# Second message-passing layer, sorted edges: node sums stored plainly by SyncE, the border node carried by a one-row matmul

## The reference

```python
hid = silu(edge_scalars @ fc_w1 * _inv(R))              # R = 64
w = hid @ fc_w2 * _inv(FC_HID)                          # 224 weights per edge
w1, w2, w3, w4, w5 = split(w, [64, 128, 160, 192], axis=-1)
es, ev = h_s[edge_src], h_v[edge_src]                   # rows gathered by source node
e0, e1 = edge_attr[:, :1], edge_attr[:, 1:4]
m_s1 = w1 * es * e0
m_s2 = w4 * einsum('eci,ei->ec', ev, e1) * _inv(3)
m_v1 = (w2 * es)[:, :, None] * e1[:, None, :]
m_v2 = w3[:, :, None] * ev * e0[:, :, None]
m_v3 = w5[:, :, None] * cross(ev, e1[:, None, :]) * _inv(2)
agg_s = segment_sum(concatenate([m_s1, m_s2], -1), edge_dst, n)     # 96 numbers per node
agg_v = segment_sum(concatenate([m_v1, m_v2, m_v3], 1), edge_dst, n)  # 128 x 3 per node
```

## Time and profile before

| | |
|---|---|
| runs, median (lowest, highest) | 3804.27 us (3803.56, 3806.49) |
| the profiled execution | 3801.2 us |
| its span, first to last instruction | 3799.6 us |
| TensorE busy | 3507.5 us (92%) |
| VectorE busy | 3493.0 us (92%) |
| ScalarE busy | 3048.0 us (80%) |
| GpSimd busy | 2571.1 us (68%) |
| mean granted TensorE clock | 0.978 |

### The profile page before, as it was taken

How to read it: one execution, slowest core, us unless ns; L and a number is a source line. 1 busy time by engine, 2 the same in 40 slices (tenths; PEclk the granted TensorE clock), 3 DMA queues, 4 the chain that set the end, 5 groups by cost and what they waited for, 6 DMA issues and landing times. The chain is left out here.

```text
span 3799.6 us, 96198 instructions
## 1 busy us (share of the span) xinstructions
PE 3507.5 (92%) x21340; PEld 2637.2 (69%) x21340; DVE 3493.0 (92%) x11954; ACT 3048.0 (80%) x11217; POOL 2571.1 (68%) x2474
## 2 busy tenths in 40 slices
PE   4999999999999999999999957977999999999997
PEld 3888888888888888888888847875333333333335
DVE  5999999999999999999999987876999999999995
ACT  4888888888888888888888856765878777878774
POOL 1777777777777777777777721112777777777772
PEclk8999999999999999999999978997999999999999
DMA  4333333333333333333333359982333433343434
GB/s 111 90 97 96 93 98 94 94 97 94 95 96 94 96 94 94 97 95 94 96 96 93 97 159 264 274 239 69 94 95 95 96 94 95 96 94 94 96 94 116
DMA packets 311032, 414.62 MB, mean 109 GB/s; under 512 B 112692, under 2 KB 245684, under 8 KB 310708
## 3 DMA queue, kind: packets, MB, share of 16 engines
q0 software_dynamic: 127568, 211.04, 24.8%
q1 hardware_dynamic: 183396, 202.83, 17.0%
HBM read 312.70 MB, written 100.94 MB: 109 GB/s over the span
## 5 line engine op out<-in xcount | busy, mean ns | idle before, releaser
L669 POOL DMA_INDIRECT ACC<-src_tab,idx x784 | 832.9, 1062 | 312.2 <-issue 238.6
L669 POOL DMA_INDIRECT TAB<-dst_tab,idx x784 | 829.2, 1058 | 238.9 <-issue 238.9
L736 POOL DMA_INDIRECT ACC<-hid_tab,idx x784 | 808.4, 1031 | 243.5 <-issue 242.9
L815 PE MATMUL TR<-ident,M 128*128 128x128 f32 x4704 | 665.2, 278 | 34.4 <-DVE M L1547 6.8
L1141 ACT ACTIVATE MT<-TR 128x768 f32<-128x768 f32 x784 | 610.3, 861 | 3.9 <-PE TR L815 3.9
L815 PEld LDWEIGHTS TR<-ident,M 128*128 128x128 f32 x4704 | 521.6, 141 | 127.4 <-DVE M L1547 127.3
L1130 ACT ACTIVATE ACC<-W,ACC 128x64 f32<-128x64 f32 x2352 | 595.0, 358 | 0.0
L864 PE MATMUL HP<-w_hv,MT 128*128 128x128 f32 x3136 | 520.1, 288 | 0.0
L839 PE MATMUL E<-w_mv,MT 128*128 128x128 f32 x3136 | 476.8, 275 | 0.0
L839 PEld LDWEIGHTS E<-w_mv,MT 128*128 128x128 f32 x3136 | 436.7, 191 | 0.0
L1324 ACT ACTIVATE ACC<-TR,y 128x128 f32<-128x128 f32 (+1 forms) x1568 | 417.0, 550 | 9.1 <-PE TR L999 9.1
(11 more groups left out here) (277 smaller groups left out, 7756.4 us busy)
## 6 DMA issues: line engine op xcount, KB each, us to landing
h_tab<-ACC SPq DMA_DIRECT2D x392, 160.0 KB, 2.1
SC<-h_tab SPq DMA_DIRECT2D x50, 640.0 KB, 4.8
TAB<-h_tab SPq DMA_DIRECT2D x48, 640.0 KB, 4.8
ACC<-in_e64T SPq DMA_DIRECT2D x98, 256.0 KB
ACC<-src_tab,idx POOLq DMA_INDIRECT x784
TAB<-dst_tab,idx POOLq DMA_INDIRECT x784
ACC<-hid_tab,idx POOLq DMA_INDIRECT x784, 3.7
agg_tab<-ACC POOLq DMA_DIRECT2D x49, 240.0 KB, 4.1
```

Of the source, the lines that this page charges most:

```text
L669: pool.indirect_dma_start(tile[:, v.slot8, g, :], None, table.ap(), bass.IndirectOffsetOnAxis(ap=idx[:, v.sslot, c:c + 1], axis=0))\
L736: pool.indirect_dma_start(gat1[:, v.slot8, g, :], None, hid_tab.ap(), bass.IndirectOffsetOnAxis(ap=idx[:, v.sslot, c:c + 1], axis=0))\
L815: ins = nc.tensor.transpose(to[:, b * G + g, :], Mt[:, g, lo:lo + w], ident[:, :])
```

## The change

In the sorted case, GpSimd no longer adds the window into HBM. SyncE stores it, as a plain write. Since a plain write of superchunk n+1's window would destroy the border node's sum from superchunk n, that node's partial sum is brought into superchunk n+1's own accumulation: a column `shared` holds a one at the row of superchunk n's window that is superchunk n+1's first node (all zeros if there is none), and in the last chunk of n+1 a matmul with this column as stationary operand and superchunk n's finished window `agS` as the moving one adds that one row to row 0 of the bank. VectorE copies the column into a static place once per superchunk, and computes all 49 columns once ahead of layer 1.

```diff
+            def store_mids(v, total):
+
+                if v.place or v.wide or not inside(v, total):
+                    return
+                sp.wait_ge(LB["ev"], v.sup + 1)
+                sp.sem_inc(s_passed, 1)
+                if v.sup_past(1):
+                    sp.wait_ge(LB["add"], v.sup * 16)
+                    sp.sem_inc(s_passed, 1)
+                row = sp.value_load(basei[0:1, bass.ds(v.sup, 1)], min_val=0, max_val=NP)
+                sp.dma_start(agg_tab.ap()[bass.ds(row, P), :], agS[:, v.sslot, 0:MW]).then_inc(LB["add"], 16)
             def sp1(t, total):
                 scalars1(t + Q, total)
                 factors1(t + Q, total)
                 places1(t + Q1, total)
+                store_mids(t + -(Q1 + 5), total)
             def sp_1(sups, wide):
-                loop_steps(sp, Q1, sups, wide, Q1, 0, sp1)
+                loop_steps(sp, Q1, sups, wide, Q1, 6, sp1)
...
-                ins = add_rows(v, total, LB, agg_tab, agS, MW, flying)
+                ins = add_rows(v, total, LB, agg_tab, agS, MW, flying) if v.wide else None
...
+                if v.place == Q1 - 1 and v.sup_past(1) and not v.wide:
+
+                    pe.wait_ge(LB["ev"], v.sup)
+                    nc.tensor.matmul(AG[v.sslot][0:1, 0:MW], shared1[:, v.sslot:v.sslot + 1], agS[:, 1 - v.sslot, 0:MW],
+                                     start=False, stop=False)
                 for g in range(G):
...
+            ch.step(TT(shared[:, 1:NS1], nbase[:, 0:NS1 - 1], nbase[:, 1:NS1], ALU.subtract))
+            ch.step(TS(shared[:, 1:NS1], shared[:, 1:NS1], nodecon[:, 0, 0:1], None, ALU.is_equal))
...
+                if v.place == 0 and v.sup_past(1) and not v.wide:
+                    nc.vector.tensor_copy(shared1[:, v.sslot:v.sslot + 1], shared[:, bass.ds(v.sup, 1)])
```

More of the change, by code:

```diff
@@ L246, in program @@
         wide = sb("wide", [P, 1])
+        shared = sb("shared", [P, NS1])
+        shared1 = sb("shared1", [P, 2])
         flag = sb("flag", [1, 1], I32)
```

## The result

The change makes the kernel a little slower: 3810.71 us median (3806.71 to 3824.63, 18 runs) against 3805.43 us (3799.88 to 3808.83, 18 runs) of the kernel before on the same chips. The ratio of the mean times is 1.0015, 95% interval 1.0009 to 1.0022, so about 6 us; the medians lie 5.3 us apart. Forecast were 3807.2 us. The profiled execution after takes 3810.5 us with a span of 3808.8 us, against 3801.2 and 3799.6 before.

A forecast was written before the change was run, and what follows sets the result against it. The prediction took GpSimd as full, its late gathers stalling VectorE, with TensorE next. Terms 4.1 + 0.4 + 0 - 2.4 + 0.8 = +2.9 us gave 3804.1 us on the profiled execution, 3807.2 on the median; range 3798 to 3824.

The forecast's parts named there:

- TensorE is what is late next, at 21.65 us: Per superchunk, once GpSimd is freed: TensorE needs 21.65 us, VectorE alone 21.21, against 22.36 before.
- The store is worth up to 33 us: Sum moved off GpSimd: at most 0.71 us per superchunk, 33 us over 47; at least nothing if stalls stay.
- The matmul lies bare in TensorE's queue: One-row matmul ahead of the last chunk's sums, unhidden: 0.80 us per superchunk, making 22.45 us, +4.1 us over 47.
- The narrow tile's new start: Rival: the next sum behind the one-row matmul starts anew, 1.0 us per matmul, 3817 us; chance 0.12.
- GpSimd is full and gets ahead: GpSimd needs 21.8 of 22.36 us per superchunk, 20.0 without the sum; it then issues gathers up to two microseconds earlier.
- SyncE's queue costs nothing: Loads behind the store's wait: second scalars' load some 4 us later, put at nothing, bounds -5 and +5 us.
- The end: From the last window's copy to the reading back: plain store instead of adding one, -2.4 us, between -2.9 and -0.9.
- the bare matmul: At the layer's end the new matmul stands bare behind the last products: +0.8 us.
- the two steps ahead of layer 1: Two small VectorE steps of 49 columns each in a serial chain ahead of layer 1: +0.4 us.
- The free matmul: Rival: the one-row matmul is next to free, TensorE's 21.65 us rule, about 3769 us; chance 0.10.
- Stalls that stay: Rival: scalars' load keeps gathers late at place 1, matmul on top; 3813 to 3820 us, up to 3842; chance 0.18.
- The number: Whole-kernel forecast: +2.9 us on the profiled 3801.2 gives 3804.1, on the median 3807.2 us; chance 0.58.

The follow-up runs named there:

- the half-column matmul: Changed kernel with the one-row matmul over 240 of the 480 columns, the border node's other columns left out of the carry: 3794.52 us, one run.
- the wide operand: Changed kernel with a stationary operand of 128 columns, 127 of them zero, in place of one column: 3804.76 us, ratio 1.0011.

## Why the prediction was right

The mechanism was right: the store frees GpSimd, VectorE's stall goes, TensorE is next, and the matmul lies bare in its queue. That the figure came so near is in part luck, as the last point says.

- *TensorE is what is late next, at 21.65 us.* Shown. The store without the matmul gives 21.78 us, against 21.65 read from one undisturbed superchunk; 0.07 of the difference are the 2.8 us in 900 that TensorE still waits for products.
- *The store is worth up to 33 us.* Shown in mechanism and near in size: 29.9 us between the medians, with the layer's end.
- *The matmul lies bare in TensorE's queue.* Shown: place 7 grows by 0.89 us, and no other distance grows. The term of the sum that was mis-sized is this one: 0.80 us were taken, of a range from 0.70 to 1.0. Over 47 superchunks the 0.09 us are 4.2 us, of the 6.1 us by which the stretch lies over its forecast (+10.2 against +4.1); the other 0.04 us per superchunk are not broken down. Without the matmul the superchunk is 0.80 and not 0.89 us shorter (22.58 against 21.78), since TensorE's wait for products, 0.07 us, comes back.
- *The narrow tile's new start.* The prediction held it to be a rival at 0.2 us above the 0.80, and named a start over 0.85 us later as its sign. The 0.89 us are over that sign: this rival is half true, at 0.10 us, by the half-column matmul and the wide operand. Its own rows had said so. The estimate "perhaps 0.1 us" is worked out there as 2.39 - 4 x 0.40 - 0.58, which is 0.21; if each of the two changes of form in a chunk has half of it, one is 0.1. The rule cited there of the Trainium skill ("TensorE: Matmul & The Clock Gate", "Step-by-step: what each phase is for"), that the number of moving columns sets the time, agrees with 0.40 us less for 240 columns less; the fixed 0.10 us come on top of it.
- *GpSimd is full and gets ahead.* Shown, but its load was put too low, 21.8 us with the sum and 20.0 without. The prediction's own 1047 us over 47 superchunks are 22.3 us: there was no slack of half a microsecond. The gathers of the changed kernel take 1.04 us in the mean and not 0.95 (780.1 us for 752), with 0.30 ahead of each 21.4 us per superchunk. So without the sum GpSimd is only 0.2 to 0.3 us quicker than TensorE's 21.65. And the sum itself costs GpSimd 1.03 us and not 1.33, as the 0.30 us behind it belong to the next gather, which has them anyway.
- *SyncE's queue costs nothing.* Shown as far as the waits go: no engine waits for the scalars' load.
- *The end:* -2.4 forecast, -1.7 measured (4.27 against 5.95). The row number took 0.9 us as forecast; from the store's issue to the reading back are 3.39 us, where 2.6 were taken. And +0.8 for the bare matmul, +0.8 measured in the last superchunk. The +0.4 for the two steps ahead of layer 1 can't be seen: window 0 comes 0.5 us earlier.
- *The rivals.* The free matmul is out by place 7 and by the half columns. Its 3769 us follow from 33 + 2.4 - 0.4 us less, not from the "3.1 + 0.4" that its text gives. Stalls that stay are out by the waits.
- *The number.* From trace to trace the sum was +2.9 us and +9.2 came. The forecast for the changed kernel on the profiled execution, 3804.1, is 6.6 us short of the median of 3810.7. It became 3807.2 because 3.1 us were added, the excess of the old kernel's median over its profiled execution. The changed kernel has no such excess (3810.7 against 3810.5), so this step had no ground, and it took away half of the miss.

## What to carry to other kernels

Taking work off a full engine is worth only the distance to the next one, and what replaces it must not go into that next one's queue: here the store alone took a superchunk from 22.36 to 21.78 us, and the matmul on TensorE brought it to 22.58. If it must go there, put it where that engine waits for somebody anyway; at place 4 the same matmul costs 0.5 us and the change pays. And when a stall sits behind a suspicious load, split the load before blaming it: the stall may only move.

## What the runs showed of the hardware

- A one-column stationary operand between wider ones costs 0.10 us once. A 128-column one with 127 columns of zeros is 0.09 us cheaper from the matmul to the `fc` (2.52 against 2.61 us).
- At a granted clock of 1.00, two float32 matmuls of 480 moving columns and 128 rows stream in 1.60 us (3003.26 to 3004.86). One that makes a single row takes 0.89 us, not less than such a one, and 0.50 us with 240 columns.
- On GpSimd a DMA that adds 8 KB into HBM takes as long as one that adds 240 KB (1.01 and 1.03 us); SyncE issues the plain store of 240 KB in 0.33 us.
- Splitting a load of 256 KB with a slowest dimension of 2 into two of 64 partitions brings the landing of the gathers beside it from 3.7 to 2.6 us (medians), and the time of the kernel does not move (ratio 1.0002).
